# A four-layer graph network on one core: in its last three edge stages every step runs one to three iterations further behind the step it needs

## What is computed

```python
def _L1_gnn_ref(feat, edge_weight, beta, eps, src, dst):
    norm_h = feat / jnp.maximum(norm, 1e-12)
    e = beta[0] * edge_weight
    p = jnp.exp(e - seg_max[src])
    p = p / seg_sum[src]
    msg = norm_h[src] * p[:, None]
    agg = jax.ops.segment_sum(msg, dst, num_segments=n)
    return (1.0 + eps[0]) * feat + agg
def _L2_gnn_ref(x, edge_index, edge_attr, W1, b1, g1, be1, W2, b2, Wu, bu, gu, beu):
    msg_in = jnp.concatenate([x[row], edge_attr], axis=-1)
    h = msg_in @ W1 + b1
    h = jax.nn.gelu(_layernorm(h, g1, be1), approximate=False)
    msg = h @ W2 + b2
    agg = jax.ops.segment_sum(msg, col, num_segments=x.shape[0])
    ...
def _L3_gnn_ref(x, W, b, edge_index):
    x_i = x[dst]
    x_j = x[src]
    feat = jnp.concatenate([x_i, x_j - x_i], axis=-1)
    msg = feat @ W.T + b
    out = jax.ops.segment_max(msg, dst, num_segments=x.shape[0])
    return jnp.where(jnp.isfinite(out), out, 0.0)
...
x = _layernorm(x + _L1_gnn_ref(x, edge_weight, L1_gnn_beta, L1_gnn_eps, src, dst), axis=-1)
```

## The kernel before

| stage | PE | DVE | ACT |
|---|---|---|---|
| L1 | back i-4, picks, T i-2 (L1536) | scan i-3, less and scale i-2 (L1553, L1555), cuts, one-hots (L1421) | first copy, back i-4, exp i-2 (L1611), cuts, one-hots |
| L2 | T i-13 (L1763), C i-2 (L1775, L1776), W i-14 (L1785), back i-16 | t i-3 (L1805), scan i-15, D i-12 (L1819) | gelu i-13 (`act_r`, L1844), back i-16, squares i-3 (L1854) |
| L3 | back i-4, T i-2 (L2039), picks (L2021) | scan i-3, one-hots | back i-4, one-hots |

## Time and profile before

### The profile page before, as it was taken

How to read it: one execution, slowest core, us unless ns; L and a number is a source line. 1 busy time by engine, 2 the same in 40 slices (tenths; PEclk the granted TensorE clock), 3 DMA queues, 4 the chain that set the end, 5 groups by cost and what they waited for, 6 DMA issues and landing times.

```text
span 6569.6 us, 82192 instructions
## 1 busy us (share of the span) xinstructions
PE 4450.2 (68%) x23151; PEld 3207.6 (49%) x23151; DVE 4209.6 (64%) x10600; ACT 3575.7 (54%) x12191; POOL 4343.1 (66%) x3819
## 2 busy tenths in 40 slices
PE   2776766766676766626777774477777764778875
PEld 1665655655565655514444443245554442444443
DVE  3876776766666777656666666266666655656655
ACT  0766666666666666625556554255555543444443
POOL 3688888888888888836666664466666634666654
PEclk7878788788878787758899997699899987998997
DMA  6766666666666666535565553366666633444543
GB/s 180 177 161 161 161 163 163 165 160 162 163 161 160 160 160 162 117 81 138 157 159 158 158 158 104 117 180 176 173 178 178 180 110 81 126 124 129 136 124 98
DMA packets 911857, 978.19 MB, mean 149 GB/s; under 512 B 103812, under 2 KB 721450, under 8 KB 910874
## 3 DMA queue, kind: packets, MB, share of 16 engines
q1 hardware_dynamic: 676730, 617.42, 32.3%
q0 software_dynamic: 234656, 355.35, 25.8%
HBM read 664.65 MB, written 307.73 MB: 148 GB/s over the span
## 4 chain that ended last, share of the span: by engine, by line
POOL 30%; issue 17%; another core or an unknown queue 16%; DVE 13%; PE 10%; ACT 10%; DMA 3%; SPq 0%; POOLq 0%; DVEq 0%; ACTq 0%
POOL tab L1059 17%; POOL arena L1077 12%; DVE arena L1341 4%; DVE arena L1421 3%; PE PS L2021 3%; ACT arena L1854 3%; ACT arena L1436 2%; DMA tab<-arena 2%; ACT arena L1844 2%; ACT arena L1323 2%; POOL arena L1099 1%; PE PS L1314 1%; PE PS L1785 1%; ACT arena L1441 1%
## 5 line engine op out<-in xcount | busy, mean ns | idle before, releaser
L1354 POOL DMA_INDIRECT arena<-T,srcI x2112 | 2028.5, 960 | 1426.3 <-issue 572.3
L1059 POOL DMA_INDIRECT tab<-arena x784 | 1304.6, 1664 | 253.2 <-issue 217.9
L1341 DVE TENSOR_TENSOR_SCAN arena<-arena,PS 128x512 f32<-128x512 bf16 x588 | 750.1, 1276 | 811.4 <-remote 663.5
L1077 POOL DMA_INDIRECT arena<-T,srcI x784 | 862.0, 1099 | 274.6 <-issue 248.9
L1323 ACT ACTIVATE arena<-PS 128x512 f32<-128x512 f32 x588 | 349.1, 594 | 1243.9 <-remote 912.1
L776 PE MATMUL PS<-We,arena 65*128 65x256 f32 x1568 | 583.4, 459 | 332.1 <-DVE arena L818 258.6
L1515 PE MATMUL PS<-arena 128*128 128x396 bf16 x2800 | 574.3, 362 | 103.8 <-issue 39.6
L795 PE MATMUL PS<-arena 128*128 128x128 f32 x1568 | 308.4, 358 | 490.9 <-ACT arena L1006 487.6
L1421 DVE TENSOR_SCALAR arena<-PS,nodeid 128x512 bf16<-128x512 f32 x908 | 627.4, 739 | 2.2 <-PE PS L1402 2.2
L2021 PE MATMUL PS<-arena 128*128 128x512 bf16 x2400 | 590.0, 399 | 15.2 <-ACT arena L1441 14.7
L778 PE MATMUL PS<-arena 128*128 128x256 f32 x1568 | 558.4, 442 | 0.0
(11 more groups left out here) (287 smaller groups left out, 10568.2 us busy)
## 6 DMA issues: line engine op xcount, KB each, us to landing
H<-arena SPq DMA_DIRECT2D x784, 256.0 KB
arena<-keepR SPq DMA_DIRECT2D x294, 256.0 KB
...
```

Of the source, the lines that this page charges most:

```text
L1059: e.indirect_dma_start(out=tabs[k % KT], out_offset=at_rows(iA[b % 10][:, c:c + 1]), in_=X2[b % 3][:, c, :], in_offset=None, compute_op=AL ...
L1077: e.indirect_dma_start(out=Gs[b % NR][:, c, :], out_offset=None, in_=T0, in_offset=at_rows(srcI[:, CB * b + c:CB * b + c + 1])).then_inc(g ...
L1341: ins = e.tensor_tensor_scan(s[b % 2][:, h, :], kR[g % 6][:, h0:h0 + CB * P], src[h], s[(b - 1) % 2][:, h, CB * P - 1:CB * P] if b else in ...
L1354: e.indirect_dma_start(out=dst[:, c, :], out_offset=None, in_=T_tab, in_offset=at_rows(srcI[:, CB * b + c:CB * b + c + 1])).then_inc(gs.of ...
```

## The change

Lags, orders and rings in the three edge stages; no instruction computes anything else. Afterwards, in iteration `i`:

| stage | PE | DVE | ACT | rings |
|---|---|---|---|---|
| L1 | back i-8, picks, T i-5 | scan i-7, less i-3, scale i-4, cuts, one-hots | first copy, back i-9, exp i-3 | G 8, s1 3, Ob 5 |
| L2 | C i-2, back i-19, W i-15, T i-13 | t i-3, scan i-17, D i-12 | gelu i-14, back i-20, squares i-4 | G 18, s1 4, feature tiles 4 |
| L3 | picks, back i-6, T i-2 | scan i-4, one-hots | back i-7, one-hots | G 10, s1 4 |

SP's stores move back with ACT's copies, and in L2 and L3 it loads features and rows four iterations ahead. In L1 the picks of a turn go into six iterations instead of seven. `scan_dve` now waits itself for the back transpose that frees its tile. The core of the diff:

```diff
-        def scan_dve(e, b, nh, src, s, kR, ld_k, scan, op0, op1, init):
-            g, h0 = b // 2, (b % 2) * CB * P
+        def scan_dve(e, b, nh, src, s, kR, ld_k, scan, B, op0, op1, init):
+            g, h0, n = b // 2, (b % 2) * CB * P, len(s)
+            if b >= n:
+                e.wait_ge(B.of(0), B.at(b - n))
             if b % 2 == 0:
                 e.wait_ge(ld_k.of(g), ld_k.at(g))
             if b >= 1:
                 e.wait_ge(scan.of(0), scan.at(b - 1))
             for h in range(nh):
-                ins = e.tensor_tensor_scan(s[b % 2][:, h, :], kR[g % 6][:, h0:h0 + CB * P], src[h],
-                                           s[(b - 1) % 2][:, h, CB * P - 1:CB * P] if b else init, op0, op1)
+                ins = e.tensor_tensor_scan(s[b % n][:, h, :], kR[g % 6][:, h0:h0 + CB * P], src[h],
+                                           s[(b - 1) % n][:, h, CB * P - 1:CB * P] if b else init, op0, op1)
             ins.then_inc(scan.of(0), 1)
...
-            NR = 6
+            NR = 8
+            NO = 5
...
-            s1 = [arena.get(1, CB * P) for _ in range(2)]
-            Ob = [arena.get(CB, P) for _ in range(NOB)]
+            s1 = [arena.get(1, CB * P) for _ in range(3)]
+            Ob = [arena.get(CB, P) for _ in range(NO)]
...
-                    if 0 <= i - 4 < NBAT:
-                        back_sp(e, i - 4, H1, Ob, O_, so)
-                    if 0 <= i - 6 < NBAT and i % 2 == 0:
-                        cut_store(e, (i - 6) // 2)
-                last_stores(e, so)
+                    if 0 <= i - 10 < NBAT:
+                        back_sp(e, i - 10, H1, Ob, O_, so)
+                    if 0 <= i - 8 < NBAT and i % 2 == 0:
+                        cut_store(e, (i - 8) // 2)
+                last_stores(e, so, NO)
...
-                j, s = pk.turn(i - pk.lag - 1)
-                if j is None:
+
+                j, s = divmod(i - 2, pk.M)
+                if s == pk.M - 1 or not 0 <= j < pk.n:
...
-                for n in pk.blocks(s):
+                for n in range(NBLK * s // (pk.M - 1), NBLK * (s + 1) // (pk.M - 1)):
...
-                for i in range(NBAT + 4):
+                for i in range(NBAT + 8):
                     pk.pe_spread(e, i)
-                    if 0 <= i - 4 < NBAT:
-                        back_pe(e, i - 4, 1, bank(3), s1, scan, B, O_)
-                    if i == 1:
+                    if 0 <= i - 8 < NBAT:
+                        back_pe(e, i - 8, 1, bank(3), s1, scan, B, O_)
+                    if i == 2:
                         e.wait_ge(cutD.of(0), cutD.at(1))
...
-                    b = i - 2
-                    if 0 <= b < NBAT:
-                        e.wait_ge(D.of(0), D.at(b))
-                        if b >= 2:
-                            e.wait_ge(scan.of(0), scan.at(b - 2))
-                        for c in range(CB):
-                            ins = e.transpose(bank(b % 2)[:, c * P:(c + 1) * P], rows_of(b)[:, c, 0:P], ident[:, :])
-                        ins.then_inc(T.of(0), 1)
+                    if 0 <= i - 5 < NBAT:
+                        pe_T(e, i - 5)
...
-                for i in range(NBAT + 5):
+                for i in range(NBAT + 7):
+                    b = i - 7
+                    if 0 <= b < NBAT:
+                        e.wait_ge(T.of(0), T.at(b))
+                        scan_dve(e, b, 1, [bank(b % 2)], s1, kR, ld_k, scan, B, ALU.mult, ALU.add, 0.0)
+                    if 0 <= i - 3 < NBAT:
+                        dve_less(e, i - 3)
+                    if 0 <= i - 4 < NBAT:
+                        dve_scale(e, i - 4)
+                    if 0 <= i - 5 < NBAT and (i - 5) % 2 == 0:
+                        dve_cut_r(e, (i - 5) // 2)
+                    if 0 <= i - 7 < NBAT and (i - 7) % 2 == 0:
+                        dve_cut_3(e, (i - 7) // 2)
+                    pk.dve_onehot(e, i)
                     if i - 2 in by_pe:
                         dve_sum(e, i - 2)
...
+                for i in range(NBAT + 9):
+                    if i - 2 in by_pe:
+                        j = (i - 2) // pk.M
                         e.wait_ge(pk.picked.of(0), pk.picked.at(j))
-                        e.activation(rows_of(b), psP[:, :, 0:XW], ACT.Copy).then_inc(first.of(0), 1)
-                    if 0 <= i - 4 < NBAT:
-                        back_act(e, i - 4, bank(3), Ob, B, O_, so)
+                        e.activation(rows_of(i - 2), psP[:, :, 0:XW], ACT.Copy).then_inc(first.of(0), 1)
+                    if 0 <= i - 9 < NBAT:
+                        back_act(e, i - 9, bank(3), Ob, B, O_, so)
+                    b = i - 3
...
-            NR = 14
+            NR = 18
...
-                for i in range(NBAT + 16):
+                for i in range(NBAT + 19):
+                    if 0 <= i - 2 < NBAT:
+                        pe_C(e, i - 2)
+                    if 0 <= i - 19 < NBAT:
+                        back_pe(e, i - 19, 1, bank(6), s1, scan, B, O_)
+                    if 0 <= i - 15 < NBAT:
+                        pe_W(e, i - 15)
                     if 0 <= i - 13 < NBAT:
                         pe_T(e, i - 13)
-                    if 0 <= i - 2 < NBAT:
-                        pe_C(e, i - 2)
-                    if 0 <= i - 14 < NBAT:
-                        pe_W(e, i - 14)
-                    if 0 <= i - 16 < NBAT:
-                        back_pe(e, i - 16, 1, bank(6), s1, scan, B, O_)
...
                     if 0 <= i - 3 < NBAT:
                         dve_t(e, i - 3)
-                    b = i - 15
+                    b = i - 17
                     if 0 <= b < NBAT:
                         e.wait_ge(W.of(0), W.at(b))
-                        if b >= 2:
-                            e.wait_ge(B.of(0), B.at(b - 2))
-                        scan_dve(e, b, 1, [bank(4 + b % 2)], s1, kR, ld_k, scan, ALU.mult, ALU.add, 0.0)
...
-                for i in range(NBAT + 16):
-                    if 0 <= i - 13 < NBAT:
-                        act_r(e, i - 13)
-                    if 0 <= i - 16 < NBAT:
-                        back_act(e, i - 16, bank(6), Ob, B, O_, so)
-                    if 0 <= i - 3 < NBAT:
-                        act_sq(e, i - 3)
+                for i in range(NBAT + 20):
+                    if 0 <= i - 14 < NBAT:
+                        act_r(e, i - 14)
+                    if 0 <= i - 20 < NBAT:
+                        back_act(e, i - 20, bank(6), Ob, B, O_, so)
...
-            NR = 6
+            NR = 10
...
-                for i in range(NBAT + 4):
+                for i in range(NBAT + 6):
                     pk.pe_spread(e, i)
-                    if 0 <= i - 4 < NBAT:
-                        back_pe(e, i - 4, 1, bank(3), s1, scan, B, O_)
+                    pe_pick(e, i)
+                    if 0 <= i - 6 < NBAT:
+                        back_pe(e, i - 6, 1, bank(3), s1, scan, B, O_)
                     if i - 2 in turn_of:
...
-                    pe_pick(e, i)
...
-                for i in range(NBAT + 3):
-                    b = i - 3
+                for i in range(NBAT + 4):
+                    b = i - 4
...
-                for i in range(NBAT + 4):
-                    if 0 <= i - 4 < NBAT:
-                        back_act(e, i - 4, bank(3), Ob, B, O_, so)
+                for i in range(NBAT + 7):
+                    if 0 <= i - 7 < NBAT:
+                        back_act(e, i - 7, bank(3), Ob, B, O_, so)
```

100 lines of the change are left out of this document (51 added, 49 removed).

## The result

The changed kernel takes 6614.6 us, median of 11 runs (6598.1 to 6625.7). The kernel before takes 6568.6 us beside it. The ratio is 1.006, its 95% interval 1.0045 to 1.0075. I had forecast 6510 us, faster by 60 us, with a range of 6330 to 6650. The time lies in the range, but the sign was wrong. What came about is the way of rival B, the loop of L2, at a price of +92 us where B at its full price had +214. Rival A falls, since no stage reached POOL's pace, and C as well: L1's gain was real.

A forecast was written before the change was run, and what follows sets the result against it. POOL was the nearest bound in every stage, pausing because PE's signals come late while gathers run unbroken. L1 -84, L2 +10 and L3 +14 sum to -60 us, giving 6510 us, with a range of 6330 to 6650.

The forecast's parts named there:

- rival B: L2: transpose signals held until the gathers land, 6.9 us a batch, +214 us, total 6713 us; chance 0.18 for slower this way.
- the loop of L2: L2: transposes, gelu, copy, back transpose and second product wait on each other in every iteration, 5.30 us a turn.
- Rival A: All three stages: depth works as meant, reaching POOL's pace or L2's loop, together -466 us, 6103 us; chance 0.06.
- C: Same time: L1 stays at two batches to a pause, only long pauses shorten, -35 us; total 6571 us; chance 0.25.
- What bounds the kernel, and why POOL pauses: Edge stages: POOL is the nearest bound; unbroken gathers make PE's signals late, starving it of buffers, two batches then a pause.
- L1, -84 forecast: L1: three batches to a pause, 56 pauses of 2.3 us instead of 83, -97 us; longer end +9 and +4.
- L2, +10 forecast: L2: pace -33 us, longer hold at the start +14, longer end +29; bounds -69 to +214.
- The end came out too: L2's end: the last 18 batches leave at 5.3 us each instead of 14 at 3.03 and 4 at 5.94, +29 us.
- the pace with late signals: L2: 5.75 us a batch, between 5.30 and 6.9, against 5.94 before; 177 batches give -33 us.
- The signs by which I would have called myself wrong: POOL's waits for PE below 120 us in L3, or L2's pace outside 5.5 to 6.1 us.
- L3, +14 forecast: L3: no gain from pauses, bounds 0 and -198 us; 4.8 more iterations at the end, less four pauses spared at the start.
- the one PSUM bank keeps the pauses: L3: the back transpose's single bank makes PE wait for ACT's copy of the batch before; gain of the pauses 0.

## Why the prediction was wrong, by its steps

**What bounds the kernel, and why POOL pauses.** Right where signals are late, and shown: the pauses are signals held while gathers run without a break. The rule of the Trainium skill that speaks against it (SBUF, State Buffer, section Who interferes with whom) was given as a reason for rival A. It is a rule on SBUF ports, and no run here shows a port that was fought over. A memset on POOL, which touches nothing of PE's, took POOL's waits for PE from 644 to 399 us, and two of them to 0.8. So DMA issued by POOL did delay PE's consumers here. The other rule of the Trainium skill given for A (Perfetto Trace Analysis, section Optimization Strategy) says that a repeating gap can mean too few buffers. Here the gap repeated, and the ring of 18 did not shorten it: it cost 25 us by the medians.

**L1, -84 forecast, -71 measured.** POOL's pauses over 0.6 us add up to 129.3 us; I had written 129. The factors behind it were not right. I took 56 pauses of 2.3 us, and there are 67 of 1.93 (in a later run of L1's part 81 of 1.7): the pauses became shorter more than rarer. That the product came out to the microsecond was luck. The end did not get longer (31.8 us from the last gather's start, against 32.2; forecast +13). Instead the gathers themselves took 1013 ns each instead of 982, +21 us, which I had not foreseen.

**L2, +10 forecast, +92 measured. This is the step that failed.** The loop was read off rightly: 5.33 us where signals are prompt, 5.30 forecast. The end came out too (+31.5, forecast +29). But the pace with late signals, which I put at 5.75 us by a choice between 5.30 and 6.9, is 6.09: +23 us instead of -33. That is 56 of the 82 us. My reason for the low value was that runs of one batch hold signals less than runs of two. In the trace of before that was so: in L2's 27 runs of one batch 6 of 46 recorded signals of PE are more than 0.3 us late, in its 76 runs of two 301 of 457, and the mean is 0.2 against 2.1 us. In the changed kernel it is 202 of 360 in runs of one batch, and the mean is 1.0 us: less than after two batches, but far from prompt. The loop has no slack to take that up. The signals of the transposes, which stand in the loop, are recorded 0.7 us late on average (127 of 196 recorded). My estimate from this is 5.33 + 0.7 = 6.0 us a batch, near the 6.09 measured. POOL pauses after almost each single batch, 175 times, 271 us: four gathers take 4.7 us from the first start to the last end and a pause 1.4 us on average (without the first, 28.4 us). 6.09 is also the point from which I had written that rival B decides. The rest is the start: the first copy comes 37 us later, forecast +14. I had counted the longer hold there, but not that the deeper pipeline has to be filled while one batch after another waits 19 us for a signal. The signs by which I would have called myself wrong (a pace in L2 outside 5.5 to 6.1 us, POOL's waits for PE in L3 below 120 us) were set too wide: neither came about. L2's window within 40 us of 1230, which I had named as a sign of being right, did fail: it is 1322.

The end came out right by luck. Counted from POOL's last gather it is 124.3 us against 55.5: 24 batches were still to be copied out and not 17, because the copy now stands seven iterations behind the transpose and not three, which I had not counted. And the last turns are longer than I had foreseen. The last iterations of L2 in the changed kernel:

```profile
5320.86 1.45 ACT L1857 ACTIVATE arena<-PS,cols 128x512 f32<-128x512 f32 x2 [5.10 <-PE PS L1778]
...
5322.20 0.59 ACT L1323 ACTIVATE arena<-PS 128x512 f32<-128x512 f32 x1
...
5322.94 0.77 PE L1314 MATMUL PS<-ident,arena 128*128 128x128 f32 x4 [2.12 <-ACT arena L1323]
...
5323.50 3.48 PE L1800 MATMUL PS<-arena,wA 128*128 128x512 f32 x4
...
5326.81 1.04 PE L1778 MATMUL PS<-ident,arena 128*128 128x128 f32 x8
...
5327.89 1.45 ACT L1857 ACTIVATE arena<-PS,cols 128x512 f32<-128x512 f32 x2 [5.09 <-PE PS L1778]
```

```profile
5275.00:5295.00 20.00, 14.21 (x84) 9.43 (x84) 16.24 (x25) 12.79 (x39) 0.00 (x0) 1.00 0.23 69
5295.00:5315.00 20.00, 14.56 (x48) 8.21 (x47) 9.36 (x19) 7.89 (x23) 0.00 (x0) 0.74 0.23 66
```

From gelu to gelu it is 7.03 us, not 5.3: the product takes 3.3 us from its start to the transposes (5323.50 to 5326.81) where it took 1.72. The granted clock was full (1.00) from 5275 to 5295. The last of the bf16 products is at 5288. From 5294.84 PE waits 2.1 us in each turn of the loop, and the mean fell to 0.74, between the levels of 1.2 and 2.4 GHz. Before, the clock stayed at 0.98 to 1.00 over the last 80 us of L2.

**L3, +14 forecast, +32 measured** (+37 in a second pair of profiles, 41 by the medians). The end is as forecast: 33.1 us after the last gather against 14.3, +19, and I had +19 for it. What I subtracted did not come. I took 5 us off for four pauses spared at the start; 65 pauses are left of 68, but they add up to 214 us (200 before), and the gathers end 14 us later instead of 5 sooner. How much of that belongs to the change is open, since the same kernel had 174 us of pauses in its second profile. That the one PSUM bank keeps the pauses, through PE's wait for ACT's copy (199.7 us, 164.9), fits these rows and remains argued.
